# Building the scan's input of states 13 and 15 from transposed dt·u, and nine of sixteen C products on GpSimd

## What is computed

```python
u  = conv(x_normed @ in_proj_w[:512].T) + conv_b          # (8, 1024, 512)
dt = clip(sigmoid(u @ dt_w.T + dt_b), 1e-4, 1)
B, C = u @ B_w.T, u @ C_w.T                                # 16 states each
# scan over time, per channel and state n:
state[n] = exp(dt * A[n]) * state[n] + dt * u * B[n] + 1e-6
y = sum_n state[n] * C[n] + D * u
out = (y * silu(z)) @ out_w.T
```

## Time and profile before

| | us |
|---|---|
| median of 3 runs | 2837.58 (2836.22 to 2841.64) |
| the profiled execution | 2837.99 |
| its span, first to last instruction | 2836.2 |
| mean granted TensorE clock | 0.957 of full speed |

### The profile page before, as it was taken

How to read it: one execution, slowest core, us unless ns; L and a number is a source line. 1 busy time by engine, 2 the same in 40 slices (tenths; PEclk the granted TensorE clock), 3 DMA queues, 4 the chain that set the end, 5 groups by cost and what they waited for, 6 DMA issues and landing times.

```text
span 2836.2 us, 48476 instructions
## 1 busy us (share of the span) xinstructions
PE 2515.6 (89%) x15232; PEld 2200.4 (78%) x15232; DVE 2229.7 (79%) x4890; ACT 2030.7 (72%) x4675; POOL 2237.1 (79%) x1354
## 2 busy tenths in 40 slices
PE   7788888888888898988898888889887699999998
PEld 4777877777777788877787777778776488888887
DVE  2999999999999999999999999999996233333332
ACT  2888888888888888888888888888884133333332
POOL 1999999999999999999999999999994133333333
PEclk9899999999999999999999999999996899999999
DMA  4222222222222222222222322222220588888886
GB/s 177 76 82 88 79 80 87 79 80 104 88 83 82 95 79 87 87 79 80 87 80 83 105 83 83 84 94 80 87 80 15 158 199 200 202 201 202 201 200 153
DMA packets 138181, 309.62 MB, mean 109 GB/s; under 512 B 15040, under 2 KB 79680, under 8 KB 137792
## 3 DMA queue, kind: packets, MB, share of 16 engines
q1 hardware_dynamic: 110848, 270.03, 30.7%
q0 software_dynamic: 27072, 36.46, 6.5%
HBM read 258.42 MB, written 48.01 MB: 108 GB/s over the span
## 4 chain that ended last, share of the span: by engine, by line
PE 40%; DVE 34%; ACT 14%; issue 9%; DMA 1%; POOL 1%; DVEq 0%; SPq 0%; POOLq 0%; ACTq 0%
PE bank L667 13%; DVE bank L1248 13%; PE bank L685 9%; DVE room L1248 8%; PE bank L552 7%; DVE room L1257 6%; ACT room L798 6%; ACT bank L814 4%; PE bank L600 3%; PE bank L616 2%; PE bank L530 2%; PE bank L589 1%; PE bank L563 1%; PE bank L723 1%; ACT bank L856 1%
## 5 line engine op out<-in xcount | busy, mean ns | idle before, releaser
L1036 POOL TENSOR_TENSOR room<-dtu,b_all 128x1024 f32<-128x1024 f32 x512 | 1205.7, 2375 | 18.3 <-DVE dtu L1425 13.9
L798 ACT ACTIVATE room<-room,neg_a 128x256 f32<-128x256 f32 x2048 | 868.0, 497 | 0.8 <-DVE room L1214 0.8
L814 ACT ACTIVATE bank<-room,eps_col 128x512 f32<-128x512 f32 x1024 | 695.0, 682 | 234.7 <-DVE carry L1262 163.6
L600 PE MATMUL bank<-ident,room 128*128 128x128 f32 x4096 | 558.0, 284 | 169.3 <-POOL room L1025 85.6
L600 PEld LDWEIGHTS bank<-ident,room 128*128 128x128 f32 x4096 | 484.9, 146 | 225.6 <-POOL room L1025 95.1
L1248 DVE TENSOR_TENSOR_SCAN bank<-room,carry,bank 128x256 f32<-128x256 f32 x864 | 578.0, 734 | 20.6 <-ACT bank L814 20.1
L1025 POOL TENSOR_TENSOR room<-room,c_all 128x1024 f32<-128x1024 f32 x224 | 533.0, 2379 | 46.3 <-issue 28.8
L1162 POOL DMA_INDIRECT out<-room,ids x144 | 223.9, 1555 | 408.5 <-ACT room L996 183.7
L1327 DVE SCALAR_TENSOR_TENSOR hid<-hid,bank 128x256 f32<-128x256 f32 (+1 forms) x312 | 130.2, 417 | 420.3 <-ACT hid L909 374.5
L1248 DVE TENSOR_TENSOR_SCAN room<-room,carry,bank 128x256 f32<-128x256 f32 x672 | 448.2, 726 | 11.1 <-ACT bank L814 10.5
L552 PE MATMUL bank<-xnT,w_conv 128*128 128x256 f32 x3072 | 404.6, 288 | 7.0 <-ACT xnT L837 5.5
(11 more groups left out here) (150 smaller groups left out, 2948.3 us busy)
## 6 DMA issues: line engine op xcount, KB each, us to landing
b_all<-b_scratch SPq DMA_DIRECT2D x128, 512.0 KB, 4.0
c_all<-b_scratch SPq DMA_DIRECT2D x128, 512.0 KB, 5.2
room<-in_wgu SPq DMA_DIRECT2D x72, 704.0 KB, 5.8
room<-in_wd SPq DMA_DIRECT2D x72, 384.0 KB
room<-x_by_expert SPq DMA_DIRECT2D x72, 260.0 KB
x_in<-in_x SPq DMA_DIRECT2D x32, 256.0 KB, 6.0
x<-in_x SPq DMA_DIRECT2D x32, 256.0 KB, 2.7
out<-x SPq DMA_DIRECT2D x32, 256.0 KB, 4.3
```

The costliest lines, as they stand in the source:

```text
L600: last = mm(tr_bank[k][:, b * P:(b + 1) * P], v[n % VRING][:, b, k * P:(k + 1) * P], ident[:, :], is_transpose=True, start=False, stop=(n ...
L798: last = af(da[n % RING][:, b, :], dt[c.par][:, b, :], ACT.Exp, scale=neg_a[:, b, n:n + 1])
L814: af(v_slot(c, n, h)[:, :], v[n % VRING][:, 2 * h:2 * h + 2, :].rearrange("p b t -> p (b t)"), ACT.Identity, bias=eps_col[:, 0:1]).then_in ...
L1036: nc.gpsimd.tensor_tensor(out=v[n % VRING][:, :, :], in0=dtu[:, :, :], in1=row, op=ALU.mult) \
```

## The change

The inputs of states 13 and 15 are no longer made by GpSimd. TensorE transposes dt·u of a chunk (so that tokens lie on partitions), ScalarE copies it to `dtuT`, ScalarE multiplies it by B[n] as a scale per partition with 1e-6 as the bias, and TensorE transposes that back into the PSUM bank from which VectorE scans. B of these two states is loaded with tokens on partitions (`load_b_tok`). GpSimd makes no B product for them, and makes the C products of states 1 and 13, which VectorE made. `dt_times_u` moves from slot 11 to slot 10. The shared expert's hidden buffer is halved to make room. The core of the diff:

```diff
-BY_POOL = [0, 2, 4, 6, 8, 10, 12]
+BY_POOL = [0, 1, 2, 4, 6, 8, 10, 12, 13]
+TURNED = [13, 15]
@@ SyncE, between write_b and load_b
+            def load_b_tok(c):
+                sp_wait(b_written, c.index * 16 + 16)
+                sp_wait(tok_ready, inputs(c.plus(-1), 0)[1])
+                for k in range(NT):
+                    src = b_scratch[c.par, TURNED[0]:NS:2, k * P:(k + 1) * P].rearrange("n t -> t n")
+                    sp.dma_start(b_tok[c.par][:, k, :], src, allow_slow_non_contiguous=True).then_inc(b_tok_loaded, 16)
@@ TensorE
+            def turn_dtu(c, k, post):
+                pe.wait_ge(dtu_ready, c.index + 1)
+                pe.wait_ge(zs_done, (c.index + 1) * NT)
+                if post:
+                    pe.wait_ge(h_ready, units_out(post, 1))
+                wait(pe, dtuT_ready, c.index * NT + k)
+                transposes(pr_bank[1], [dtu[:, b, k * P:(k + 1) * P] for b in range(KD)]).then_inc(dtu_turned, 1)
+            def turn_state(c, n, h):
+                pe.wait_ge(tok_ready, inputs(c, n + 1)[1])
+                bank_free(*before(c, n, h))
+                for j in range(2):
+                    for k in range(NT):
+                        b = 2 * h + j
+                        last = nc.tensor.transpose(v_slot(c, n, h)[:, j * TC + k * P:j * TC + (k + 1) * P],
+                                                   v_tok[n % VRING][:, k, b * P:(b + 1) * P], ident[:, :])
+                last.then_inc(turn_ready, 1)
@@ proj_conv, half 0, j 0
+                    wait(pe, dtuT_ready, c.index * NT)
@@ TensorE's body
+                        if scan and slot == 12:
+                            turn_state(scan, 13, 1)
                         if slot == 0 and post:
                             state_transpose(post, NS - 2)
                             state_transpose(post, NS - 1)
+                        if slot == 0 and scan and post:
+                            turn_dtu(scan, 1, late_of(post))
                         if slot == 0 and late_of(post):
                             shared_down(late_of(post))
...
+                        if scan and slot + 2 in TURNED:
+                            turn_state(scan, slot + 2, 0)
+                        if proj and slot == 15:
+                            turn_dtu(proj, 0, post)
                         if post:
                             for u in units_of(slot, GU_SLOT):
                                 gate_up(post, u, w_gu, xn2T, False)
+                        if scan and slot == 14:
+                            turn_state(scan, 15, 1)
@@ ScalarE
+            def take_dtu(c, k):
+                act.wait_ge(dtu_turned, c.index * NT + k + 1)
+                af(dtuT[:, k, :], pr_bank[1][:, :], ACT.Copy).then_inc(dtuT_ready, 1)
+            def b_times_turned(c, n):
+                act.wait_ge(dtuT_ready, c.index * NT + NT)
+                act.wait_ge(b_tok_loaded, (c.index + 1) * NT * 16)
+                act.wait_ge(tr_ready, c.index * NS + n - VRING + 1)
+                i = turned_inputs(n)
+                for k in range(NT):
+                    af(v_tok[n % VRING][:, k, :], dtuT[:, k, :], ACT.Identity, scale=b_tok[c.par][:, k, i:i + 1],
+                       bias=eps_col[:, 0:1]).then_inc(tok_ready, 1)
@@ ScalarE's body (add_eps is left out for n in TURNED)
+                        if scan and slot + 2 in TURNED:
+                            b_times_turned(scan, slot + 2)
+                        if scan and post and slot == 0:
+                            take_dtu(scan, 1)
                         if norm and slot == 4:
                             norm_apply(norm)
                         if proj:
                             project(proj, slot)
...
+                        if proj and slot == 15:
+                            take_dtu(proj, 0)
@@ GpSimd's body
+                        if scan and proj and slot == 10:
+                            dt_times_u(proj)
                         n = slot + MUL_LEAD
-                        if scan and n < NS:
+                        if scan and n < NS and n not in TURNED:
@@ VectorE's scans
-                    dve.wait_ge(v_ready, halves(c, n) + h + 1)
+                    if n in TURNED:
+                        dve.wait_ge(turn_ready, inputs(c, n)[1] + (2 if n in BY_POOL else h + 1))
+                    else:
+                        dve.wait_ge(v_ready, inputs(c, n)[0] * 2 + h + 1)
```

More of the change, by code:

```diff
@@ L90, in dve_products, with turned_inputs, pool_inputs @@
     return n - pool_products(n)
+def turned_inputs(n):
+    return sum(1 for m in TURNED if m < n)
+def pool_inputs(n):
+    return n - turned_inputs(n)
 def units_of(slot, slots):
@@ L158, in build @@
         y_tok = sb("y_tok", [P, NT, DI])
+        dtuT = sb("dtuT", [P, NT, DI])
+        b_tok = [sb(f"b_tok{i}", [P, NT, len(TURNED)]) for i in range(2)]
         b_all = [sb(f"b_all{i}", [P, NEAR, TC]) for i in range(2)]
@@ L163, in build @@
         v = [room[:, i, :, :] for i in range(VRING)]
+        v_tok = [room[:, i, :, :].rearrange("p b t -> p (b t)").rearrange("p (k d) -> p k d", k=NT) for i in range(VRING)]
         da = [room[:, VRING + i, :, :] for i in range(RING)]
@@ L477, in __call__ @@
                         write_b(proj)
+                        load_b_tok(proj)
                         load_b(proj, 0)
@@ L907, in gate @@
                 act.wait_ge(gu_ready, c.index * UNITS + u + 1)
-                act.wait_ge(dn_ready, c.index + HEAD)
-                af(hid[0:rows, hid_slot(c, u), :], bank[0:rows, 0:TC], ACT.Tanh, scale=0.5).then_inc(th_ready, 1)
+                act.wait_ge(dn_ready, c.index + HEAD + (0 if tiled else 1))
+                af(hid_tile(c, u, tiled)[0:rows, :], bank[0:rows, 0:TC], ACT.Tanh, scale=0.5).then_inc(th_ready, 1)
             class Body(Phases):
@@ L939, in start @@
                     decays(Chunk(0, 0), 2)
+                    for k in range(NT):
+                        take_dtu(Chunk(0, 0), k)
                     take_normed(Chunk(0, 1))
```

48 lines of the change are left out of this document (34 added, 14 removed).

## The result

| | us |
|---|---|
| median before (4 runs, same chip) | 2837.89 (2836.22 to 2841.64) |
| median after (4 runs) | 2861.57 (2858.93 to 2864.07) |
| ratio | 1.0081, 95% interval 1.0064 to 1.0099 |
| span of the profiled execution | 2858.8, against 2836.2 |
| mean granted TensorE clock | 0.965 of full speed, against 0.957 |

The kernel became 0.8% slower, where 2834 us and a slight gain were forecast. The experts' tiles have not moved, and in the chunk loop the engines that had been the busiest are idle more. Windows of the kernel after: busy us (count) of PE, weight loads, DVE, ACT, POOL; clock; DMA.

The account below looks back on a forecast made before the run. It took the chunk loop to be bound by a cycle of DVE and PE, POOL running along. Terms of -0.3 us a chunk made -6 us, the prologue +1.9; together -4 on 2838.0 gave 2834 us, range 2812 to 2868.

Parts of the forecast that it names:

- The ring of DVE and PE: Chunk loop: DVE's part, slot 4 to state 15's end, 46.6 us, then PE's to the output product, 19.8 us.
- z late: Slot 11: two new ACT activations, 1.45 us less 0.4 of slack, delay z for DVE by 1.05 us (0.85 to 1.95).
- POOL's unchanged sum, and its floor: Chunk loop: POOL swaps two B products for two C products of equal length; its own floor is about 64 us.
- the gathers: Loads of B in 4-byte pieces, 512 a chunk: free if under 10 us; rival of 2870 us and more, 5%.
- C product of 13 off DVE: Slot 13, in DVE's part: moving state 13's C product to POOL saves 1.35 us a chunk.
- slot 11's clock, wait for the turn of 13: Slots 11 and 12: a fallen clock slows gate_up, so DVE waits for state 13's second turn, +0.3 us (0 to 0.9).
- ACT and PE lie later: Slots 5 to 9: DVE, held in slot 4, waits more for ACT's add_eps, +0.25 us a chunk (0 to 0.8).
- PE's part, with POOL's C product of 1: State 15's end to slot 4: -0.9 us on the mean; POOL's C product of state 1 takes back 0.35.
- last turn: Last turn of the chunk loop: no z follows there, so nothing moves.
- prologue: Ahead of the first scan: ACT's copies and PE's turns of dt·u delay its release by 1.9 us.
- The clock stays low: Rival: shared_down behind slot 0's transposes stays at 1.2 GHz in two thirds of the chunks, 2868 us; 28%.
- The relief gets through: Rival: slot 11's activations are hidden, DVE saves 1.35 us in both parts, 2799 us; 16%.

Follow-up runs that it names:

- c13_dve: The changed kernel with the C product of state 13 back on DVE, state 1's still on POOL: 2890.7 us, ratio 1.0183 to the kernel before.
- pad11: The kernel before plus three unread ACT activations, 1.5 us together, in slot 11 ahead of z: 2876.6 us, ratio 1.0130.
- gate_first: The changed kernel with PE's gate_up in slot 11 put ahead of the first turn of state 13: 2848.2 us, ratio 1.0031 to the kernel before.
- both_first: The changed kernel with z taken ahead of ACT's two activations and gate_up ahead of the turn of state 13: 2818.7 us, ratio 0.9928.
- c1_dve: The changed kernel with the C product of state 1 back on DVE, state 13's still on POOL: 2850.8 us, ratio 1.0037 to the kernel before.

## Why the prediction was wrong

**Right.** The ring of DVE and PE; z late by 1.05 us (1.06 measured); the pair of activations at 1.45 us to the start of what follows (1.41, from 1244.02 to 1245.43); PE's idle ahead of the turn 3.2 (3.17); `shared_down` 2.8 us and 2.0 to 2.6 behind state 15 (2.76, 2.2); state 13's product worth some 1.35 (41 us with state 1's on DVE, 29 with it on POOL); POOL's late product for state 1; POOL's unchanged sum, and its floor; the gathers, as the spread loads behind them still land in 4.0 us: the page after has the line of the earlier trace rows as it stands.

**Wrong.** The sum was -0.3 us a chunk and the measured one +0.5. By its terms:

| term, us a chunk | predicted | measured |
|---|---|---|
| C product of 13 off DVE | -1.35 | -1.3 |
| z late | +1.05 | +1.15 |
| slot 11's clock, wait for the turn of 13 | +0.3 (0 to 0.9) | +0.55 |
| ACT and PE lie later | +0.25 (0 to 0.8) | +0.55 |
| PE's part, with POOL's C product of 1 | -0.9 + 0.35 | -0.44 |
| sum | -0.3 | +0.5 |

Every large mechanism was named and every term with bounds lay inside them; the direction was lost in their middle, and no single term turns it. The first measured line is that of c13_dve's slot 13. The second is the wait, 1.06, and 0.1 because the two halves of the gate no longer overlap (0.68 + 0.69 us where the pair had 1.27); pad11's period, 1.13 longer, agrees. The fourth is not measured by itself: it is what is then left of the 0.94 by which DVE's part grew.

Two terms make up two thirds of the 0.8 us that are missing, and they are the **failed steps**. One is **the turn of state 13**, 0.55 in place of 0.3: I took a third of its range, on the ground that the clock might or might not fall. In the timeline after, the first `gate_up` of slot 11 takes over 2.4 us in 25 of 31 bodies (before, over 2.3 in 5), and DVE waits for the second turn in 18, for 0.2 to 1.8 us, and for 2.9 in the last. gate_first removes this wait and is 13 us faster.

The other is **"ACT and PE lie later"**, 0.55 in place of 0.25. The wait that it named, DVE's for bank writes, grew just as priced: 20.6 + 7.8 us against 16.6 + 7.6 from 1000 to 2000 us, 0.3 a chunk. What the term put at nothing is the rest: 0.2 of waiting for ACT's copy of a last column, which is not there in both_first and so comes from slot 11, and 0.1 of slightly longer scans. The bank writes' part hangs on the C product of state 1: DVE waits for PE in 22 of 29 bodies, TensorE's convolution follows right behind the late product, and ACT, with hardly a gap between slots 5 and 9, hands the delay on. With that product on DVE (c1_dve) the bank waits are 15.6 + 7.5 us, under those of the kernel before.

So C product 1 was mispriced as well. I had taken its 1.35 us as a gain of PE's part, by DVE's earlier arrival in slot 4. PE was only 0.8 us early before; beyond that, a faster DVE just waits. Moving the product makes PE's part 0.35 us shorter and DVE's part 0.46 longer. It was worth nothing that can be told from noise without the product of 13 beside it, and -11 us with it. That the measured time lies inside the stated range, 2812 to 2868, is no merit of the sum: the range was drawn wide enough for a slow rival by another cause, a low clock in slot 0, which did not come.

No run takes the move of `dt_times_u` to slot 10, or the halved hidden buffer, by itself; what they cost stays open.

The **last turn** was wrong too. "Nothing moves" there; it became 2.8 us longer. DVE waits in it 3.12 us for the output product and 2.93 us for a turn:

```profile
2143.98 0.69 DVE L1378 TENSOR_TENSOR x<-bank,x 128x512 f32<-128x512 f32 x1 [3.12 <-PE bank L677]
...
2176.44 2.66 DVE L1347 TENSOR_TENSOR_SCAN room<-room,carry,bank 128x256 f32<-128x256 f32 x4 [2.93 <-PE bank L661]
```

z is not in this body, but the turns are, and POOL's ninth product: from 2127 to 2192 us PE waits 8.2 us for POOL's C products in three pieces, where it waited 2.0 in the same stretch before. I had looked at z alone. And the **prologue**: the first scan's release (L1304, L1208 before) comes at 77.05 in place of 74.80, 2.25 us later where 1.9 was worked out, and the first full bodies bring it to 4.4.

**The rivals.** "The clock stays low" is ruled out where it was placed: no `shared_down` of the loop took over 3.2 us after, 19 of 29 did before. By groups, 1000 to 1520 us: busy us, mean ns.

```profile
L746 PE MATMUL bank<-w_dn,hid 128*128 128x256 f32 x62 | 16.0, 379 | 0.0
...
L728 PE MATMUL bank<-xn2T,w_gu 128*128 128x256 f32 x128 | 37.6, 447 | 0.0
```

`shared_down` had 460 ns before and has 379 now; `gate_up` had 401 and has 447. The low clock moved from slot 0 to slot 11, where an idle of 2.9 to 3.2 us stands in front of the first turn. The rule of the Trainium skill (TensorE: Matmul & The Clock Gate, Part 4) by which transposes do not count as activity in the same way is not borne out by this trace. PE's timeline between slot 14's `gate_up` and `shared_down`, in the body shown above:

```profile
1255.20 1.89 PE L728 MATMUL bank<-xn2T,w_gu 128*96 128x256 f32 x8
1256.93 0.60 PE L661 MATMUL bank<-ident,room 128*128 128x128 f32 x4
1259.30 1.09 PE L635 MATMUL bank<-ident,room 128*128 128x128 f32 x8 [1.77 <-POOL room L1120]
1260.23 0.60 PE L564 MATMUL bank<-ident,dtu 128*128 128x128 f32 x4
1260.67 1.04 PE L635 MATMUL bank<-ident,room 128*128 128x128 f32 x8
1262.01 1.09 PE L635 MATMUL bank<-ident,room 128*128 128x128 f32 x8 [0.30 <-DVE room L1356]
```

36 transposes and 2.7 us of idle, the granted clock at 1.00 from 1257 to 1264 us, and the 2.76 us of `shared_down` right behind are those of the full level, in 30 of 31 bodies. That transposes always hold the clock is not shown, though. In c13_dve the same 36 have less idle among them, 2.4 us, and `shared_down` behind them is slow:

```profile
1280.77 1.09 PE L635 MATMUL bank<-ident,room 128*128 128x128 f32 x8 [1.84 <-DVE room L1356]
1282.43 1.08 PE L564 MATMUL bank<-ident,dtu 128*128 128x128 f32 x4 [0.58 <-ACT dtuT L892]
1283.31 3.97 PE L746 MATMUL bank<-w_dn,hid 128*128 128x256 f32 x12
```

There the longer wait ends 2.5 us before `shared_down` starts, in after 4.8 us before it; whether that is the reason no run shows. "The relief gets through" is ruled out as the change stands, and shown as a possibility by both_first: with the activations hidden, 43 us are gained. The period, 66.3, came out just at the bound that I had set for being wrong.

## What to carry to other kernels

Work that is taken off the busiest engine is worth what its own place in the ring is worth: the same product gave 41 us in one slot and nothing measurable in another. What an engine is relieved of is read from its busy time afterwards (2.3 us a chunk less here, where the removed instructions are 2.7 us long). A new instruction on an engine "with time to spare" costs its length less the slack of the next thing in its list that somebody waits for; look that up first, and let the next thing go ahead. Where two engines stand in a ring with under 1 us between them, count each saving only up to that slack, and price what lies behind the engine that becomes late (its next products, and whoever runs without a gap on them) at the full delay.

## What the runs showed of the hardware

- TensorE kept the higher of its two levels over a list of 36 transposes with single idle times of up to 2.1 us between them (`shared_down` at 379 ns a matmul, in 30 of 31 bodies after). Behind 2.9 to 3.2 us of idle it mostly did not: eight matmuls of `gate_up`, 1.9 us at the higher level, took 2.8 to 3.6 us in 24 of the 30 bodies before the last. The length of one idle time does not settle it: in c13_dve, behind 1.84 and 0.58 us, `shared_down` took 3.97 us, and over 3.2 us in 22 of the 30 seen.
- An activation with a scale and a bias from memory over 128x512 takes 0.80 us alone and 1.50 as a pair; one with a bias only, 0.68.
- 512 reads of 4 bytes a chunk, 16384 in all (the packets under 512 bytes rose from 15040 to 32448), cost nothing that shows: the loads behind them land in 4.0 us as before.
